# A four-image transformer step on one Trainium2 core: expert-sum transposes in the next step, attention units of one key range, scores in 64x64 tiles

## The chip, the core and the metric

The kernel runs on one core of one Trainium2 chip. The metric is the device time of one execution in microseconds (us), lower is better. Engine names are those of the profile: PE is TensorE's matmul and PEld its weight load, DVE is VectorE, ACT is ScalarE, POOL is GpSimd, SP is the queue of SyncE.

## What is computed

128 images of 176x208 pixels become 143 patches of 16x16 and one class token each, so 144 tokens of 128 channels. Three layers follow, each with a residual: a gated causal convolution layer, a layer with eight experts of which each token takes two, and (what this case is about) windowed attention and a layer that picks one of 16 weight matrices per image:

```python
qkv = (x @ w_qkv + b_qkv).reshape(B, S, 3, H, hd)      # H = 8 heads, hd = 16
q, k, v = (qkv[:, :, 0], qkv[:, :, 1], qkv[:, :, 2])
idx = jnp.arange(S)[:, None] + jnp.arange(-w, w + 1)[None, :]   # w = 32
valid = (idx >= 0) & (idx < S)
scores = jnp.einsum('bshd,bswhd->bshw', q, k_win) * scale
scores = jnp.where(valid[None, :, None, :], scores, -1000000000.0)
attn = jax.nn.softmax(scores, axis=-1)
out = jnp.einsum('bshw,bswhd->bshd', attn, v_win).reshape(B, S, D)
return out @ w_out + b_out
...
h = h + _L1_attn_ref(_layernorm(h, axis=-1), ...)
h = h + _L1_ffn_ref(_layernorm(h, axis=-1), ...)
```

## The kernel before

It has three stages. Stage A (to about 1150 us) takes the images through the first layer and the router of the experts and writes one row per token and chosen expert to DRAM. Stage B (to about 1800 us) runs the experts over blocks of 256 rows. Stage C (the last 1,250 us) is the one that the change touches. Channels lie on the partitions, tokens on the free axis; a step handles four images, 576 tokens, so there are 32 steps.

**A step of stage C is a software pipeline over five items.** `step(v, w, x, y, z)` is called on each engine with the item that entered now (`v`) and those that entered one to four steps earlier (`w`, `x`, `y`, `z`). The loop that calls it is `single_steps` on TensorE and `c_steps` on the others. Within a step the order of the instructions on each engine is written out by hand, and engines meet through semaphores alone.

- `v`: GpSimd gathers 12 rows of 96 tokens from `expert_out` into `ycho` by indirect DMA (L1429), multiplies them by the router's weights (L1437) and adds the two experts of each token into `ysum` (L1442). TensorE transposes `ysum` with six matmuls into the PSUM tile A0 (`moe`, L1488), as the last but one thing of its step.
- `w`: VectorE adds the residual (`prec`, L1845, the second thing in its step). Two layer norms follow (TensorE L1477 and L1482, ScalarE L1693 to L1699, VectorE L1894, L1900). The last instruction of VectorE's step writes the normalized `xq` (L1918).
- `x` and `y`: attention. `query_or_key` (L1494) projects `xq`, ScalarE writes `qs` (L1703) and `keys` (L1710), `values_in` (L1502) makes the values of each image and key range.
- `z`: the last layer with the matrix that VectorE picked for each image (`pick_expert`, whose last instruction is L1941, and L1825, the residual).

**Attention units.** The queries of an image are cut in 9 blocks of 16; each block sees one of three ranges of 96 keys, which start at 0, 32 and 48 (`STARTS`, `window`). Four blocks are a unit, nine units an item: before, unit `u` holds blocks 4u to 4u+3 of the 36 in order, so most units have blocks of two or three (image, range) pairs. Per unit:

- `diagonal` (POOL, L1450) spreads the queries into `qdiag`, two heads per 32 rows, 128x128 elements. It waits until the scores of three units earlier are done (a ring of three buffers). Two gathers or one follow each diagonal but the first.
- `scores` (PE) writes the band mask into a PSUM bank (L1515), then adds 16 matmuls, 4 blocks on 4 diagonal array tiles of 32x32 (L1519). An fp32 matmul has two records in the trace, so 32.
- `minimum` (DVE, L1805), `exps` (ACT, L1725), `turn` (PE transposes, L1529), `turned` (ACT, L1733).
- `values` (PE): softmax sums (L1542) and attention times values (L1554), four matmuls for each group of blocks that share an image and a range.
- `halves` and `heads` (DVE, L1812 to L1820): reciprocal, the choice of the right head, and the product, which goes to `att`.

The end of TensorE's step before reads:

```python
if x:
    scores(x, 8)
    turn(x, 6)
if v:
    if w:
        pe.wait_ge(norm4_act, w.upto(3, 2))
    ...
    moe(v, A0)
if x:
    values(x, 5)
```

and the end of VectorE's has `halves(x, 4)`, `residual(z)` (L1825), `heads(x, 4)` (L1817, L1820), `minimum(x, 7)` and the instruction for `xq`. `values(x, 5)` waits for L1817 of unit 4. The next step of TensorE begins with the query projection, which waits for `xq_ready`.

Of the kernel before, what the change touches and what calls it, by code (L numbers as in the profile page):

```python
# [22 lines left out]
ALU = mybir.AluOpType  # L23
# [22 lines left out]
HD = D // HEADS  # L46
WIN = 32
# [26 lines left out]
def window(b):  # L74

    return next(j for j, w in enumerate(STARTS)
                if w <= max(0, b * QB - WIN) and min(S, (b + 1) * QB + WIN) <= w + KW)

# [27 lines left out]
def const_tiles():  # L106
# [3 lines left out]
    for b in range(NQB):  # L110
        q = b * QB + np.arange(128) % QB
        key = STARTS[window(b)] + np.arange(KW)
        ok = abs(key[None, :] - q[:, None]) <= WIN
        band[:, b, :][ok] = 0.0
    band = np.concatenate([band, band[:, :UB - 1]], axis=1)
# [16 lines left out]
def build(nc, images, a):  # L132
# [8 lines left out]
    with ExitStack() as ctx:  # L141
# [65 lines left out]
        parity, pair_ones = sb("parity", [128, 2]), sb("pair_ones", [KW, 2, 2 * HD])  # L207
        place = [sb(f"place{s}", [G, 2 * NG], I32) for s in range(2)]
# [983 lines left out]
        def b_vector(v):  # L1192
# [35 lines left out]
            v.tensor_reduce(parity[:], C("head_rows").rearrange("p (t j) -> p j t", j=2), AX_X, ALU.add)  # L1228
            for j in range(2):
                v.memset(pair_ones[:, j, j * HD:(j + 1) * HD], 1.0)  # L1230
                v.memset(pair_ones[:, j, (1 - j) * HD:(2 - j) * HD], 0.0)
# [60 lines left out]
        qdiag, ex = ring_c("qdiag", [128, UB, 2, QB]), ring_c("ex", [128, UB, KW])  # L1292
# [38 lines left out]
        def blocks(u):  # L1331
            return [((u * UB + b) // NQB, (u * UB + b) % NQB) for b in range(UB)]
# [4 lines left out]
        def last_use(r):  # L1337

            return max(u for u in range(NU) if any((m * NWIN + window(qb)) // UB == r for m, qb in blocks(u)))
# [78 lines left out]
        def c_pool(pool):  # L1418
# [26 lines left out]
            def diagonal(x, u):  # L1445
                if u == 0:
                    pool.wait_ge(q_ready, x.upto(1, 1))
                if u >= RING or x.old(1):
# [3 lines left out]
                    qs[x.s][:, u * UB * QB:(u + 1) * UB * QB].rearrange("p (b q) -> p b q", b=UB).unsqueeze(2)  # L1452
                    .to_broadcast([128, UB, 2, QB]),
                    parity[:].unsqueeze(1).unsqueeze(3).to_broadcast([128, UB, 2, QB]),
# [15 lines left out]
        def c_tensor(pe):  # L1470
# [28 lines left out]
            def values_in(x, r, bank):  # L1499
                for w in range(UB):  # L1500
                    m, j = (r * UB + w) // NWIN, (r * UB + w) % NWIN
# [5 lines left out]
            def scores(x, u):  # L1507
# [6 lines left out]
                b0 = (u * UB) % NQB  # L1514
# [17 lines left out]
            def values(x, u):  # L1532
                need = max(m * NWIN + window(qb) for m, qb in blocks(u)) // UB
                if u in (0, 1, 3, 5):
# [11 lines left out]
                while b < UB:  # L1546
# [5 lines left out]
                    for t in range(NT):  # L1552
                        at = slice(t * PH, (t + 1) * PH)
                        done = nc.tensor.matmul(pv_bank()[at, b:b + c], val[:, m * NWIN + j, at],  # L1554
# [237 lines left out]
        def c_vector(v):  # L1792
# [22 lines left out]
            def heads(x, u):  # L1815
# [4 lines left out]
                v.tensor_tensor(att[:, u * UB * QB:(u + 1) * UB * QB].rearrange("p (b q) -> p b q", b=UB),  # L1820
# [16 lines left out]
            def step(v_, w, x, y, z):  # L1837
# [205 lines left out]
```

## Time and profile before

| what | value |
|---|---|
| runs of the kernel | 3069.62, 3073.66, 3074.09 us (median 3073.66) |
| the profiled execution: its own time | 3065.54 us |
| its span, first to last instruction | 3063.6 us |
| mean granted TensorE clock | 0.965 of full |
| busy: PE, PEld, DVE, ACT, POOL | 91%, 71%, 65%, 60%, 43% |
| DMA | 284.73 MB, mean 93 GB/s |

The busy shares are averages over three stages with different limits. In the profile's slices stage C is the last third: TensorE at nine tenths or more, VectorE at seven, ScalarE at six, GpSimd at five, DMA at one. How a step of it runs is read from the timeline of one step on each engine.

### The profile page before, as it was taken

What the parts mean: (1) busy time and instruction counts of PE and PEld (TensorE: products, weight loads), DVE (VectorE), ACT (ScalarE), POOL (GpSimd) and SP (SyncE); (2) the same over time, 40 slices, a digit from 0 to 9 for tenths busy, and PEclk for the clock granted to TensorE, in tenths of its full rate; (3) what the DMA queues carried; (4) which work ended last, traced back from release to release, by engine and by line L of the source; (5) the groups of instructions that cost most, each with busy time, mean ns of one, the idle gap of its engine ahead of it and who ended that gap; (6) DMA issues with size and microseconds to landing.
All of it is one profiled execution on the core that took longest, in us unless ns stands there. A gap on an engine that the chain in (4) does not pass through costs nothing.

```text
span 3063.6 us, 85773 instructions
## 1 busy us (share of the span) xinstructions
PE 2778.5 (91%) x31087; PEld 2160.1 (71%) x31087; DVE 1981.9 (65%) x4482; ACT 1844.8 (60%) x3693; POOL 1314.0 (43%) x1252
## 2 busy tenths in 40 slices
PE   6999999999999994899999968999999999999997
PEld 4666666666666663799999956777777777777775
DVE  4888888888888886222222215777777777777775
ACT  4776777777677774344444435666666666666664
POOL 1355555555655555000000026555555555555540
PEclk9999999999999997999999988999999999999998
DMA  3122222222222211677777741111111111111110
GB/s 130 70 78 95 85 83 83 77 77 77 89 90 83 83 32 52 211 231 226 228 230 229 229 141 39 54 50 46 46 47 46 46 45 47 46 45 45 46 34 28
DMA packets 139576, 284.73 MB, mean 93 GB/s; under 512 B 25440, under 2 KB 82784, under 8 KB 135392
## 3 DMA queue, kind: packets, MB, share of 16 engines
q1 hardware_dynamic: 114912, 245.77, 24.9%
q0 software_dynamic: 24576, 37.80, 4.5%
q8 instruction: 54, 0.88, 0.1%
q14 instruction: 34, 0.28, 0.0%
HBM read 215.18 MB, written 68.29 MB: 93 GB/s over the span
## 4 chain that ended last, share of the span: by engine, by line
issue 26%; PE 21%; POOL 10%; DMA 2%; ACT 1%; DVE 0%; POOLq 0%; SPq 0%; DVEq 0%; ACTq 0%
POOL ycho L1429 5%; PE psum L1519 4%; PE psum L1477 3%; PE psum L1494 3%; POOL ysum L1442 3%; PE psum L1502 2%; PE psum L1542 2%; PE psum L1529 2%; DMA ycho<-expert_out,place 2%; PE psum L1554 1%; POOL qdiag L1450 1%; PE psum L1515 1%; PE psum L1572 1%; PE psum L1482 1%; POOL ycho L1437 1%
## 5 line engine op out<-in xcount | busy, mean ns | idle before, releaser
L1429 POOL DMA_INDIRECT ycho<-expert_out,place x384 | 358.9, 935 | 664.7 <-issue 651.3
L1013 POOL DMA_INDIRECT expert_in<-rows,slot_i x384 | 445.3, 1160 | 130.5 <-issue 108.0
L1182 ACT ACTIVATE hid<-psum,w_blk 128x256 f32<-128x256 f32 x608 | 268.9, 473 | 326.9 <-PE psum L1139 326.9
L1725 ACT ACTIVATE ex<-psum,smin 128x96 f32<-128x96 f32 x1152 | 295.3, 341 | 158.2 <-DVE smin L1805 155.2
L483 PE MATMUL psum<-xn,w_in 128*128 128x288 f32 x1024 | 299.3, 416 | 31.7 <-ACT rf L697 27.7
L1450 POOL TENSOR_TENSOR qdiag<-qs,parity 128x128 f32<-128x128 f32 x288 | 117.7, 414 | 422.8 <-PE psum L1519 267.1
L1148 PE MATMUL psum<-w_blk,hid 128*128 128x128 f32 x2432 | 296.7, 275 | 0.0
L1812 DVE RECIPROCAL inv<-psum 128x64 f32<-128x64 f32 x288 | 159.0, 552 | 209.4 <-PE psum L1554 209.3
L1139 PE MATMUL psum<-x_t,w_blk 128*128 128x256 f32 x1216 | 289.5, 381 | 2.2 <-DMA w_blk<-w_exp_in 2.2
L989 POOL TENSOR_TENSOR unit<-unit 128x576 f32<-128x576 f32 x64 | 129.3, 2021 | 370.3 <-ACT unit L650 262.6
L1148 PEld LDWEIGHTS psum<-w_blk,hid 128*128 128x128 f32 x2432 | 283.9, 192 | 0.1
L483 PEld LDWEIGHTS psum<-xn,w_in 128*128 128x128 f32 x1024 | 187.2, 191 | 101.0 <-DVE xn L836 40.5
L1519 PE MATMUL psum<-keys,qdiag 32*32 32x96 f32 x9216 | 248.6, 244 | 0.0
L1519 PEld LDWEIGHTS psum<-keys,qdiag 32*32 32x32 f32 x9216 | 186.6, 104 | 76.5 <-issue 76.4
L1139 PEld LDWEIGHTS psum<-x_t,w_blk 128*128 128x128 f32 x1216 | 212.8, 191 | 34.2 <-DMA w_blk<-w_exp_in 2.6
L1733 ACT ACTIVATE ex_t<-psum 96x512 f32<-96x512 f32 x288 | 170.9, 593 | 106.4 <-PE psum L1529 106.2
L1246 DVE COPY x_t<-psum 128x256 f32<-128x256 f32 x152 | 64.5, 424 | 230.4 <-PE psum L1130 230.4
L1254 DVE TENSOR_TENSOR rows_out<-psum,w_blk 128x256 f32<-128x256 f32 x152 | 64.5, 424 | 215.8 <-PE psum L1148 215.8
L489 PE MATMUL psum<-xin,w_tok 128*128 128x286 f32 x768 | 195.0, 411 | 2.2 <-DVEq L453 2.2
L1805 DVE TENSOR_REDUCE smin<-psum 128x4 f32<-128x384 f32 x288 | 159.0, 552 | 49.9 <-PE psum L1519 48.6
L1529 PE MATMUL psum<-cst,ex 128*96 128x128 f32 x1152 | 180.0, 279 | 4.0 <-ACT ex_t L1733 2.0
L489 PEld LDWEIGHTS psum<-xin,w_tok 128*128 128x128 f32 x768 | 144.8, 192 | 50.6 <-issue 11.4
(237 smaller groups left out, 6031.7 us busy)
## 6 DMA issues: line engine op xcount, KB each, us to landing
w_blk<-w_exp_in SPq DMA_DIRECT2D x152, 578.0 KB, 4.0
xin<-x_in SPq DMA_DIRECT2D x32, 1716.0 KB, 7.2
rows_in<-expert_in SPq DMA_DIRECT2D x152, 128.0 KB, 2.4
expert_out<-rows_out SPq DMA_DIRECT2D x152, 128.0 KB, 3.3
h_dram<-h SPq DMA_DIRECT2D x32, 288.0 KB
x_dram<-x SPq DMA_DIRECT2D x32, 288.0 KB, 2.1
h1c<-h_dram SPq DMA_DIRECT2D x32, 288.0 KB, 3.0
x2c<-x_dram SPq DMA_DIRECT2D x32, 288.0 KB, 3.3
```

The costliest lines, as they stand in the source:

```text
L483: last = nc.tensor.matmul(bank[:, g, 0:T2], w, two(src)[:, g, :], start=True, stop=True)
L489: last = nc.tensor.matmul(bank[:, g, 0:2 * NPATCH], w_tok[:, k, :], xin[x.s][:, k, g * 2 * NPATCH:(g + 1) * 2 * NPATCH], start=(k == 0), s ...
L1013: pool.indirect_dma_start(out=expert_in[:, :], out_offset=bass.IndirectOffsetOnAxis(ap=slot_i[z.s][:, n:n + 1], axis=0), in_=rows[z.s][:, ...
L1139: nc.tensor.matmul(HB[b.s][c % HK], w_blk[b.q][:, c * 128:(c + 1) * 128], x_t[b.s][:], start=True, stop=True).then_inc(hid_done[b.s], 1)
L1148: last = nc.tensor.matmul(YB[b.s][:, t * 128:(t + 1) * 128], hid[b.s][:, c, t * 128:(t + 1) * 128], w_blk[b.q][:, FF + c * D:FF + (c + 1) ...
L1182: nc.scalar.activation(hid[b.s][:, c, :], HB[b.s][c % HK], ACT.Gelu_apprx_tanh, bias=w_blk[b.q][:, FF + FC * D + c:FF + FC * D + c + 1]).t ...
L1429: pool.indirect_dma_start(out=ycho[x.s][:, k, :], out_offset=None, in_=expert_out[:, :], in_offset=bass.IndirectOffsetOnAxis(ap=place[x.s] ...
L1519: done = nc.tensor.matmul(bank[at, b * KW:(b + 1) * KW], qdiag[u % RING][at, b, :, :].rearrange("p j q -> p (j q)"), keys[at, m, key_range ...
L1529: done = nc.tensor.transpose(XB[0:KW, b * 128:(b + 1) * 128], ex[u % RING][:, b, :], C("ident"))
L1725: done = nc.scalar.activation(ex[u % RING][:, b, :], score_bank(u)[:, b * KW:(b + 1) * KW], ACT.Exp, bias=smin[u % RING][:, b:b + 1], scal ...
L1733: nc.scalar.activation(ex_t[u % RING][:].rearrange("p b r -> p (b r)"), XB[0:KW, :], ACT.Copy).then_inc(ext_ready, 1)
L1805: v.tensor_reduce(smin[u % RING][:], score_bank(u).rearrange("p (b k) -> p b k", b=UB), AX_X, ALU.min).then_inc(min_ready, 1)
```

## The change

Three things are changed in stage C:

1. **The transposes of `ysum` (`moe`) move to the next step**, behind `values(y, 8)` and ahead of `scores(x, 1)`, for item `w` instead of `v`. `scores(x, 2)` follows `scores(x, 1)` at once and the small matmul `gates` comes after it. VectorE's `prec` moves behind the heads of unit 8.
2. **Units of one key range.** Units 0 to 7 are blocks 0 to 3 and 5 to 8 of each image, unit 8 is block 4 of all four images. `STARTS` stays; block 5 now takes the range at 48. Values are stored in the order `PLACES`, and the band mask in the order of `block_order`.
3. **Scores in 64x64 tiles.** `qdiag` holds four heads per 64 rows (`QH = 4`), 128x256 elements, masked by the new constant `quad` in place of `parity`. A unit has 4 blocks on 2 diagonal tiles of 64x64, 8 matmuls instead of 16.

```diff
+QH = 4
...
 def window(b):
-    return next(j for j, w in enumerate(STARTS)
-                if w <= max(0, b * QB - WIN) and min(S, (b + 1) * QB + WIN) <= w + KW)
+    return 0 if b < UB else 1 if b == UB else 2
...
+def block_order():
+    return list(range(UB)) + list(range(UB + 1, NQB)) + [UB] * IMGS
...
-        qdiag, ex = ring_c("qdiag", [128, UB, 2, QB]), ring_c("ex", [128, UB, KW])
+        qdiag, ex = ring_c("qdiag", [128, UB, QH, QB]), ring_c("ex", [128, UB, KW])
...
         def blocks(u):
-            return [((u * UB + b) // NQB, (u * UB + b) % NQB) for b in range(UB)]
+            if u == NU - 1:
+                return [(m, UB) for m in range(IMGS)]
+            return [(u // 2, (u % 2) * (UB + 1) + b) for b in range(UB)]
+
+        def unit_columns(t, u):
+            if u == NU - 1:
+                return four(t)[:, :, UB * QB:(UB + 1) * QB]
+            at = (u // 2) * S + (u % 2) * (UB + 1) * QB
+            return t[:, at:at + UB * QB].rearrange("p (b q) -> p b q", b=UB)
+
+        PLACES = [(m, j) for m in range(IMGS) for j in (0, 2)] + [(m, 1) for m in range(IMGS)]
...
                 pool.tensor_tensor(
                     qdiag[u % RING][:],
-                    qs[x.s][:, u * UB * QB:(u + 1) * UB * QB].rearrange("p (b q) -> p b q", b=UB).unsqueeze(2)
-                    .to_broadcast([128, UB, 2, QB]),
-                    parity[:].unsqueeze(1).unsqueeze(3).to_broadcast([128, UB, 2, QB]),
+                    unit_columns(qs[x.s][:], u).unsqueeze(2)
+                    .to_broadcast([128, UB, QH, QB]),
+                    quad[:].unsqueeze(1).unsqueeze(3).to_broadcast([128, UB, QH, QB]),
...
                 for b, (m, qb) in enumerate(blocks(u)):
-                    for t in range(NT):
-                        at = slice(t * PH, (t + 1) * PH)
+                    for t in range(HEADS // QH):
+                        at = slice(t * QH * HD, (t + 1) * QH * HD)
...
                     query_or_key(x, 0, A1)
-                    if w:
-                        pe.wait_ge(prec_ready, w.upto(1, 1))
                     values_in(x, 0, A0)
...
                 if y:
                     values(y, 8)
+                if w:
+                    if x:
+                        pe.wait_ge(k_ready, x.upto(1, 1))
+                    moe(w, A0)
                 if x:
                     scores(x, 1)
+                    scores(x, 2)
+                if w:
+                    pe.wait_ge(prec_ready, w.upto(1, 1))
                 if z:
                     gates(z, A0)
-                if x:
-                    scores(x, 2)
...
                     scores(x, 8)
                     turn(x, 6)
-                if v:
-                    if w:
-                        pe.wait_ge(norm4_act, w.upto(3, 2))
-                    elif v.old(1):
-                        pe.wait_ge(prec_ready, v.upto(1, 0))
-                    moe(v, A0)
                 if x:
                     values(x, 5)
...
-                if w:
-                    v.wait_ge(moe_done, w.upto(1, 1))
-                    v.wait_ge(h_landed[w.s], 32 * w.n + 32)
-                    v.tensor_tensor(two(prec[:]), both(A0), two(x2c[w.s][:]), ALU.add).then_inc(prec_ready, 1)
...
                     heads(y, 8)
+                if w:
+                    v.wait_ge(moe_done, w.upto(1, 1))
+                    v.wait_ge(h_landed[w.s], 32 * w.n + 32)
+                    v.tensor_tensor(two(prec[:]), both(A0), two(x2c[w.s][:]), ALU.add).then_inc(prec_ready, 1)
```

TensorE's order across the end of a step before: the band and score matmuls of unit 8 (L1515, L1519), `turn(x, 6)` (L1529), the transposes of `ysum` (L1488), `values(x, 5)` (L1542, L1554), then the next step's query projection (L1494):

```order
L1515 MATMUL psum<-band,ident_h 128x384
L1519 MATMUL psum<-keys,qdiag 32x96 x16
L1529 MATMUL psum<-cst,ex 96x128 x4
L1488 MATMUL psum<-cst,ysum 128x96 x6
L1542 MATMUL psum<-ex_t,pair_ones 32x64 x8
L1554 MATMUL psum<-ex_t,val 32x64 x8
```

In the changed kernel the transposes no longer stand there. They stand early in the step, where lines are shifted (L1563 and L1575 are `values`, L1509 the transposes, L1536 and L1540 `scores`, L1587 `gates`):

```order
L1563 MATMUL psum<-ex_t,pair_ones 32x64 x8
L1575 MATMUL psum<-ex_t,val 32x32 x16
L1507 ISA
L1509 MATMUL psum<-cst,ysum 128x96 x6
L1533 REGISTER_ALU
L1536 MATMUL psum<-band,ident_h 128x384
L1540 MATMUL psum<-keys,qdiag 64x96 x8
L1533 REGISTER_ALU
L1536 MATMUL psum<-band,ident_h 128x384
L1540 MATMUL psum<-keys,qdiag 64x96 x8
L1586 ISA
L1587 MATMUL psum<-gdiag,cst 128x4
```

They come behind `values(y, 8)`, whose four blocks now have four groups of 32 columns, and the score units 1 and 2 run back to back, each with 8 matmuls.

## Rows read from the trace of the kernel before

**Rows 1.** The page's first line.
```profile
span 3063.6 us, 85773 instructions
```
**Rows 2.** Table by stretch: length, busy time (instructions) of five engines, PE clock, DMA.
```profile
2200.00:2400.00 200.00, 187.49 (x3729) 141.17 (x3729) 147.72 (x366) 121.93 (x324) 110.35 (x120) 0.96 0.16 46
```
**Rows 3.** The list of waits, 2200 to 2600: us in total, times, longest.
```profile
POOL qdiag L1450 <- PE psum L1519: 78.8, 42, 3.8
...
PEld psum L1488 <- POOL ysum L1442: 25.9, 11, 2.4
```
**Rows 4.** Single lines, 2131 to 2960; L1442 in 1800 to 1950: ns min/median/max, first and last.
```profile
L1437 POOL TENSOR_TENSOR ycho<-ycho,weights x23: 2747/2749/2751, 2131.6 to 2956.9; 96x1536 f32<-96x1536 f32 x23
...
L1941 DVE TENSOR_SCALAR l<-l,m x23: 2540/2683/2752, 2131.6 to 2957.1; 4x16 f32<-4x16 f32 x23
...
L1442 POOL TENSOR_TENSOR ysum<-ycho x5: 1795/1803/2194, 1827.6 to 1949.1; 96x768 f32<-96x768 f32 x5
```
**Rows 5.** Timeline of PE, one step: start, us, instruction, [idle before <-releaser].
```profile
2362.07 0.71 PE L1488 MATMUL psum<-cst,ysum 96*128 96x96 f32 x6 [2.00 <-POOL ysum L1442]
...
2363.66 2.29 PE L1494 MATMUL psum<-xq,w_qkv 128*128 128x288 f32 x4
...
2389.30 0.43 PE L1542 MATMUL psum<-ex_t,pair_ones 96*32 96x64 f32 x16
...
2399.68 0.72 PE L1488 MATMUL psum<-cst,ysum 96*128 96x96 f32 x6 [2.17 <-POOL ysum L1442]
```
**Rows 6.** Timeline of POOL, the same step.
```profile
2389.48 0.40 POOL L1450 TENSOR_TENSOR qdiag<-qs,parity 128x128 f32<-128x128 f32 x1 [2.17 <-PE psum L1519]
...
2393.96 2.75 POOL L1437 TENSOR_TENSOR ycho<-ycho,weights 96x1536 f32<-96x1536 f32 x1 [1.76 <-DMA ycho<-expert_out,place]
2396.78 2.84 POOL L1442 TENSOR_TENSOR ysum<-ycho 96x768 f32<-96x768 f32 x1
```
**Rows 7.** Timeline of DVE, the same step.
```profile
2398.19 1.52 DVE L1820 TENSOR_TENSOR att<-one_head,inv 128x64 f32<-128x64 f32 x1
...
2400.10 0.74 DVE L1918 TENSOR_TENSOR xq<-psum,r 128x576 f32<-128x576 f32 x1
```
**Rows 8.** Timelines of DVE, POOL and PE, the step that ends at 2102.
```profile
2096.16 0.21 DVE L1941 TENSOR_SCALAR l<-l,m 4x16 f32<-4x16 f32 x1
...
2099.83 1.51 DVE L1820 TENSOR_TENSOR att<-one_head,inv 128x64 f32<-128x64 f32 x1
...
2096.21 2.78 POOL L1437 TENSOR_TENSOR ycho<-ycho,weights 96x1536 f32<-96x1536 f32 x1 [1.83 <-DMA ycho<-expert_out,place]
...
2101.32 0.72 PE L1488 MATMUL psum<-cst,ysum 96*128 96x96 f32 x6 [1.63 <-POOL ysum L1442]
...
2102.59 1.23 PE L1494 MATMUL psum<-xq,w_qkv 128*128 128x288 f32 x4
...
2126.97 0.43 PE L1542 MATMUL psum<-ex_t,pair_ones 96*32 96x64 f32 x16
```
**Rows 9.** Table by stretch, columns as in rows 2, behind the transposes of two steps.
```profile
2362.50:2366.00 3.50, 3.50 (x42) 2.59 (x41) 3.01 (x9) 1.52 (x6) 0.00 (x0) 0.55 0.74 252
...
2101.30:2105.00 3.70, 3.68 (x54) 3.09 (x54) 3.46 (x10) 2.43 (x7) 0.23 (x1) 1.00 0.77 247
```
**Rows 10.** PE from 2371.31 to 2371.40; then the chain that ended last: start, us, what.
```profile
2371.32 0.28 PE L1519 MATMUL psum<-keys,qdiag 32*32 32x96 f32 x4
...
2333.67 0.27 PE psum L1515
2333.94 0.79 PE psum L1519 x32
...
2336.14 0.23 PE psum L1554 x16
...
2343.15 0.22 PE psum L1554 x8
...
2344.54 0.16 PE psum L1515
```

More of the change, by code:

```diff
@@ L113, in const_tiles @@
         ok = abs(key[None, :] - q[:, None]) <= WIN
+        assert STARTS[window(b)] <= max(0, b * QB - WIN) and min(S, (b + 1) * QB + WIN) <= STARTS[window(b)] + KW
         band[:, b, :][ok] = 0.0
-    band = np.concatenate([band, band[:, :UB - 1]], axis=1)
+    band = band[:, block_order()]
     parts = {
@@ L207, in build @@
         parity, pair_ones = sb("parity", [128, 2]), sb("pair_ones", [KW, 2, 2 * HD])
+        quad = sb("quad", [128, QH])
         place = [sb(f"place{s}", [G, 2 * NG], I32) for s in range(2)]
@@ L1228, in b_vector @@
             v.tensor_reduce(parity[:], C("head_rows").rearrange("p (t j) -> p j t", j=2), AX_X, ALU.add)
+            v.tensor_reduce(quad[:], C("head_rows").rearrange("p (t j) -> p j t", j=QH), AX_X, ALU.add)
             for j in range(2):
@@ L1331, in blocks, with place_of @@
         def blocks(u):
-            return [((u * UB + b) // NQB, (u * UB + b) % NQB) for b in range(UB)]
+            if u == NU - 1:
[7 more added lines that the diff above has]
+        PLACES = [(m, j) for m in range(IMGS) for j in (0, 2)] + [(m, 1) for m in range(IMGS)]
+        def place_of(m, qb):
+            return PLACES.index((m, window(qb)))
         def key_range(qb):
@@ L1337, in last_use @@
         def last_use(r):
-            return max(u for u in range(NU) if any((m * NWIN + window(qb)) // UB == r for m, qb in blocks(u)))
+            return max(u for u in range(NU) if any(place_of(m, qb) // UB == r for m, qb in blocks(u)))
         class Single:
@@ L1500, in values_in @@
                 for w in range(UB):
-                    m, j = (r * UB + w) // NWIN, (r * UB + w) % NWIN
+                    m, j = PLACES[r * UB + w]
                     last = nc.tensor.matmul(bank[0:KW, 0, w * D:(w + 1) * D],
@@ L1513, in scores @@
                 bank = score_bank(u)
-                b0 = (u * UB) % NQB
+                b0 = 2 * UB if u == NU - 1 else (u % 2) * UB
                 nc.tensor.matmul(bank, ident_h[:], band[:, b0 * KW:(b0 + UB) * KW], start=True, stop=False)
                 for b, (m, qb) in enumerate(blocks(u)):
-                    for t in range(NT):
-                        at = slice(t * PH, (t + 1) * PH)
+                    for t in range(HEADS // QH):
+                        at = slice(t * QH * HD, (t + 1) * QH * HD)
                         done = nc.tensor.matmul(bank[at, b * KW:(b + 1) * KW],
@@ L1532, in values @@
             def values(x, u):
-                need = max(m * NWIN + window(qb) for m, qb in blocks(u)) // UB
-                if u in (0, 1, 3, 5):
+                need = max(place_of(m, qb) for m, qb in blocks(u)) // UB
+                if u in (0, 4, 8):
                     pe.wait_ge(val_ready, x.upto(NWIN, need + 1))
@@ L1553, in values @@
                         at = slice(t * PH, (t + 1) * PH)
-                        done = nc.tensor.matmul(pv_bank()[at, b:b + c], val[:, m * NWIN + j, at],
+                        done = nc.tensor.matmul(pv_bank()[at, b:b + c], val[:, PLACES.index((m, j)), at],
                                                 ex_t[u % RING][:, b:b + c, at].rearrange("p b (j q) -> p b j q", j=2),
@@ L1819, in heads @@
                 v.wait_ge(head_step, x.upto(HEAD * NU, HEAD * u + 3))
-                v.tensor_tensor(att[:, u * UB * QB:(u + 1) * UB * QB].rearrange("p (b q) -> p b q", b=UB),
+                v.tensor_tensor(unit_columns(att[:], u),
                                 one_head[:], inv[:], ALU.mult).then_inc(att_ready, 1)
```

## Prediction

> **What bounds the kernel now.** The profiled execution took 3065.54 us with a span of 3063.6 [rows 1], 8.1 us under the median of the three runs; I add my difference to the median, 3073.66. The change touches stage C only, the last 1,200 us. There TensorE is busy 187.5 us of 200 [rows 2], so the first thing to find is what its last 12.5 us wait for. The list of waits gives it: over 400 us TensorE's weight load stood 11 times, 25.9 us, before the expert-sum transposes, until GpSimd had written `ysum` [rows 3]. That is 2.4 us per step of four images. A step lasts 37.51 us: 23 products of the expert rows (L1437) start from 2131.6 to 2956.9, 825.3 / 22 [rows 4].
>
> The step is a loop. Take the one that ends at 2401. Let Q be the start of its query projection (2363.66) and s5 the end of its sixth score unit, where the next work starts (2389.30) [rows 5]. The timeline shows no gap between them: Q to s5 is 25.64. GpSimd's last diagonal waits for that unit; two gathers and their landing follow, and the product starts at 2393.96, s5 + 4.66 [rows 6]. The sum follows, and TensorE, done with `turn(x, 6)` and idle for 2.17, starts the transposes at 2399.68, 5.72 after the product began [rows 5]. From transposes to the next query it is 1.59 (2362.07 to 2363.66) [rows 5]. 25.64 + 4.66 + 5.72 + 1.59 = 37.61, the period of that step.
>
> Two more things are in these rows. First, VectorE is stopped by GpSimd: L1941, on 4x16 elements, takes 2683 ns as median of 23 [rows 4] and 0.21 in the one step where it began before the product [rows 8]; the product of 2.75 us covers it. L1820 takes 1.52 and ends with the sum [rows 7]. **`xq` is written two VectorE instructions later**, at 2400.10 plus 0.74 [rows 7]. Second, the idle time costs TensorE's clock: granted 0.55 just behind it, in 2362.5 to 2366, against 1.00 at the same place of the step at 2101.3 [rows 9], where it had been idle 1.63 us [rows 8]. So that is the 1.2 GHz level for most of the stretch, and its price is seen in Q to s5: 25.64 there, 2126.97 - 2102.59 = 24.38 in the other [rows 5, 8], 1.26 us; from transposes to Q it is 1.59 here and 2102.59 - 2101.32 = 1.27 there, another 0.32. In all 1.6.
>
> **The change, part by part.**
>
> *64x64 score tiles.* The instructions per unit go from 16 to 8 (records from 32 to 16), and one might book half of 0.79 us [rows 10]. But the records start in fours: in the first 0.09 us of a unit four have started [rows 10], one on each diagonal tile, and the fifth only later. A record streams the same 96 columns before and after, and each tile then has four blocks times two records, 8 in a row, in both kernels. 0.79 less about 0.11 of draining (0.27 to the first score record where the 0.16 of the same band matmul suffices elsewhere [rows 10]) is 0.68, or 8 x 0.085. Two tiles of 64x64 run 8 records each just as long. The weight load grows from 32 to 64 columns, but the transposes of `ysum` load 128 columns before moving 96, six in 0.72 with the tail [rows 5], so a load is hidden. I take **0**. Bounds: issue-bound, so down to half, -0.39; two tiles not side by side, +0.68. The first value is nearest to the fours seen. The Trainium skill, TensorEngine Tiling (Array Packing), section Instruction Overhead, gives about 60 cycles per matmul; as an estimate that is 32 x 25 ns = 0.80 per unit, as if the present unit were bound by issuing, and the new one would be bound by its columns. By it a unit would gain 0.1; the fours speak against it. This is a rival below.
>
> *Units of one key range.* The attention-times-value matmuls go from 18 groups to 12 per step. A unit of one group (8 records) takes 0.22, one of two groups (16) 0.23 [rows 10]: the columns are the same, four tiles share them. I take 0, at most -0.02 a unit; the last unit, with four groups, 0 to +0.2. Query columns are read at another stride, same length. The value tiles are released later (the second after unit 7, was 5), still before ScalarE comes to them.
>
> *Diagonals.* Nine GpSimd instructions per step grow from 128 to 256 elements. 0.40 now [rows 6]; the sum on 768 took 1.80 undisturbed [rows 4], so (1.80 - 0.40) / 640 = 2.19 ns per element: +0.28. By the product's slope (2.75 for 1536, 1.7 ns) +0.21, by doubling +0.40. GpSimd waits for scores 78.8 us in 11 steps [rows 3], 7.2 per step, and that hides eight of them (2.2 us; without the cover they would cost it). **One is on the path: the ninth, behind s5, +0.28.**
>
> *The transposes in the next step.* They leave the end of the step, and stand between `values(y, 8)` and `scores(x, 1)`, some 11 us later, long after the sum. The wait for `ysum` is gone, and the 0.72 moves into Q to s5: six records of 96 columns, 0.50 (0.45 to 0.72). Behind them `prec` (0.74 on VectorE, moved behind the heads of unit 8) must be ready before the gates, which now come after two score units of 1.05 each: 2.1 us against about 1.5, no wait. `minimum(x, 1)` is 0.7 later and is needed 2 us after that by `turn(x, 1)`; no cost.
>
> But what is late next? The query projection needs `xq`, and that stands on VectorE behind L1820, which ends with the sum. **So the wait for `ysum` is replaced by one for `xq`, about as late.** The product comes 0.28 later and L1941 then starts some 0.26 before it, so I take the other step's path: product 2096.21, query 2102.59, 6.38, with L1941 at 0.21, and L1820 at 1.51 again, ending with the sum at 2101.34 [rows 8]. The Trainium skill, SBUF — State Buffer, section SBUF: two separate sides, calls it an exclusive lock of the ports that VectorE and GpSimd share, held by whichever began first for its whole instruction; both steps agree.
>
> Sum at full clock: Q to s5 24.38 + 0.50, s5 to product 4.66 + 0.28, product to Q 6.38: 36.20. The same pieces of now, at full clock, are 24.38 + 4.66 + 5.72 + 1.27 = 36.03. TensorE is idle longer than now: it ends `turn` at 2399.68 - 2.17, s5 + 8.2, waits for VectorE's L1817 to run `values(x, 5)`, and waits again to s5 + 11.3, some 3 us in all less 0.6 of work. So the clock falls. It costs up to 1.6; but the fall may come before Q, and what passes at 1.2 GHz while nothing runs is free: down to 1.0. **37.2 to 37.8, middle 37.5 against 37.51.** Over 27 steps that are full (the five before are shorter and bound alike) -8 to +8 us; I put -2.
>
> **Rivals.**
> 1. *Scores bound by issuing.* 0.13 less for each of six units on the path, 0.8 per step, -21 us: 3052. For it: 0.79 / 32 is 25 ns. Against: the fours. 0.11.
> 2. *The clock stays up*, because the 0.6 of `values(x, 5)` cuts the idle time in two. 36.2, -1.3 x 27 = -35: 3038. For: the step at 2101 kept it after 1.63 us idle [rows 8, 9]. Against: 2.2 us sufficed 22 times, and now the two pieces together are longer. 0.13.
> 3. *VectorE isn't stopped*, so `xq` is early, and TensorE runs through: 37.51 - 2.2 idle - 1.6 clock + 0 = 33.7 by TensorE, but GpSimd's loop (4.94 + 4.6 behind s5) holds it at about 34.5, -3 x 27 = -80: 2993. Against: 23 of 23 steps. 0.07.
> 4. *Slower: L1941 stays behind the product.* It decides whether the product starts before it; now it does by 0.02. Then the sum takes 2.84 as now [rows 6], `xq` ends at product + 6.9 and Q is 0.6 later; with the clock's 1.6 the step is 38.4, +0.9 x 27 = +24: 3098. For: it is so in 23 steps, and VectorE's chain may slip with the longer diagonals. 0.15.
> 5. *The two 64x64 tiles don't overlap*: +0.68 on six units, 4.1 per step, +110: 3184. It is also how a change that doesn't do what it says would look. 0.05.
>
> **The numbers.** The forecast has 0.49: 3071.7, its own range 3065 to 3082. The range for 8 in 10 takes in rivals 1, 2 and 4: 3030 to 3101; rivals 3 and 5 stay out. 0.2% is 6 us, about what a measurement of this kernel can tell from no change. Faster: 0.31 of rivals 1 to 3 and 0.07 of the forecast's edge, 0.38. Slower: 0.20 and 0.06, 0.26. Same 0.36.
>
> **What would show it.** Right: products 37.2 to 37.8 apart; no wait of TensorE for `ysum`, and one of about 2 us before the query projection (L1515 after), released by VectorE's `xq`; a score unit still 0.79 and its records 0.28 for the first two or so; the diagonal 0.61 to 0.80; granted clock low once in each step. Wrong: a score unit under 0.7 (rival 1), clock at 1.00 throughout (2), no wait before the query (3), L1941's successor at 2.7 (4), a unit near 1.4 (5).

## The result, and the profile after

The changed kernel takes 3094.56 us (median of 6 runs, 3089.14 to 3099.66), the kernel before 3072.32 beside it (6 runs, 3067.89 to 3074.09). The ratio is 1.0075, 95% interval 1.0065 to 1.0086: slower by 0.75%. That is above the forecast's own range, 3065 to 3082, and inside the range for 8 in 10, 3030 to 3101; of the three directions "slower" had been given the smallest chance. The profiled execution took 3092.34 us, 26.8 more than that of before, with a span of 3090.5.

The products (L1458, L1437 before) start 38.52 us apart, 22 periods from 2134.6 to 2982.1; before it was 37.5 [rows 4]. One more microsecond in each of about 27 full steps is 27 us, the whole of the difference between the two profiled executions.

First the list of waits of the changed kernel, 2200 to 2600, in the columns of [rows 3]:

```profile
POOL qdiag L1471 <- PE psum L1540: 80.1, 41, 3.4
...
PEld psum L1515 <- DVE xq L1936: 23.1, 10, 2.3
...
PEld psum L1563 <- DVE one_head L1835: 9.2, 11, 0.9
```

The wait for `ysum` (25.9 us in [rows 3]) is gone. A wait for `xq` of 2.3 us per step (2.04 on the matmul side) stands in its place, and one of 0.8 (0.6) in front of `values(x, 5)`. That exchange was forecast. Next the timeline of TensorE over one step, as in [rows 5]:

```profile
2368.09 0.43 PE L1563 MATMUL psum<-ex_t,pair_ones 96*32 96x64 f32 x16 [0.53 <-DVE one_head L1835]
...
2370.77 2.29 PE L1515 MATMUL psum<-xq,w_qkv 128*128 128x288 f32 x4 [2.04 <-DVE xq L1936]
...
2382.41 0.71 PE L1509 MATMUL psum<-cst,ysum 96*128 96x96 f32 x6
...
2398.56 0.43 PE L1563 MATMUL psum<-ex_t,pair_ones 96*32 96x64 f32 x16
...
2407.42 0.43 PE L1563 MATMUL psum<-ex_t,pair_ones 96*32 96x64 f32 x16 [0.61 <-DVE one_head L1835]
...
2410.10 1.70 PE L1515 MATMUL psum<-xq,w_qkv 128*128 128x288 f32 x4 [2.04 <-DVE xq L1936]
```

Q is 2370.77, s5 is 2398.56, the next Q 2410.10: 27.79 and 11.54, where the step in [rows 5] had 25.64 and 11.97. GpSimd's timeline (as in [rows 6]) and VectorE's (as in [rows 7]) show the 11.54:

```profile
2398.73 0.61 POOL L1471 TENSOR_TENSOR qdiag<-qs,quad 128x256 f32<-128x256 f32 x1 [1.76 <-PE psum L1540]
2399.49 0.94 POOL L1450 DMA_INDIRECT ycho<-expert_out,place  x1
2400.74 1.36 POOL L1450 DMA_INDIRECT ycho<-expert_out,place  x1 [0.30 <-issue]
2403.80 2.75 POOL L1458 TENSOR_TENSOR ycho<-ycho,weights 96x1536 f32<-96x1536 f32 x1 [1.70 <-DMA ycho<-expert_out,place]
2406.63 2.20 POOL L1463 TENSOR_TENSOR ysum<-ycho 96x768 f32<-96x768 f32 x1
```

```profile
2403.22 0.21 DVE L1959 TENSOR_SCALAR l<-l,m 4x16 f32<-4x16 f32 x1
...
2404.43 2.74 DVE L1843 TENSOR_TENSOR outs<-outs,h 128x576 f32<-128x576 f32 x1
2407.09 0.27 DVE L1835 SCALAR_TENSOR_TENSOR one_head<-psum,parity,half 128x64 f32<-128x64 f32 x1
2407.40 1.52 DVE L1838 TENSOR_TENSOR att<-one_head,inv 128x64 f32<-128x64 f32 x1
2408.84 0.55 DVE L1823 TENSOR_REDUCE smin<-psum 128x4 f32<-128x384 f32 x1
2409.30 0.74 DVE L1936 TENSOR_TENSOR xq<-psum,r 128x576 f32<-128x576 f32 x1
```

The residual (L1843) starts during the product and ends behind it: 2.74 us for what takes 0.74 in the kernel before, where it starts behind the product. `one_head`, which `values(x, 5)` needs, stands behind it. L1838 is stopped by the sum and ends with it at 2408.8; `xq` comes two instructions later. TensorE's idle time at the end of the step looks like the shadow of these two instructions; e11_order tests that. The last gather takes 1.36 instead of 0.92 and pushes the product back.

Last, tables by stretch (columns as in rows 2): first 200 us, then two stretches behind the query of the step at 2370.77, and two behind that of 2410.10.

```profile
2200.00:2400.00 200.00, 187.05 (x2648) 138.72 (x2648) 138.09 (x354) 121.13 (x322) 115.39 (x121) 0.94 0.15 44
2370.50:2374.00 3.50, 3.23 (x10) 2.59 (x11) 1.84 (x7) 1.84 (x5) 0.00 (x0) 0.50 0.64 209
2374.00:2377.50 3.50, 3.50 (x36) 2.56 (x35) 0.76 (x3) 2.10 (x6) 3.17 (x5) 0.63 0.06 14
...
2409.90:2413.40 3.50, 3.30 (x13) 2.85 (x14) 1.76 (x7) 1.77 (x5) 0.66 (x2) 0.62 0.60 182
2413.40:2416.90 3.50, 3.50 (x43) 2.72 (x42) 1.17 (x4) 2.84 (x7) 3.05 (x4) 0.89 0.06 14
```

The clock falls about the query in each step, and in 6 of 22 steps the 1.2 GHz level lasts about twice as long (0.50 and 0.63 against 0.62 and 0.89). Those steps are 39.3 to 39.5 us, the others 38.0 to 38.4. In the six the clock fell 0.7 to 1.1 us ahead of the query, while TensorE stood idle; in the other 16 it fell between 0.6 us ahead of it and 0.9 behind.

**All steps together.** The pieces of the prediction, as means over the 22 or 23 steps with a product between 2130 and 2960, from the same rows (Q to s5, s5 to product, product to the end of `ysum`, product to the end of `xq`, product to the next Q), for the kernels that ran on chips that take about 3070 us for the kernel before:

| kernel | Q to s5 | s5 to product | to ysum | to xq | to next Q | step |
|---|---|---|---|---|---|---|
| before | 25.52 | 4.58 | 5.66 | 6.88 | 7.36 | 37.45 |
| changed | 27.02 | 5.21 | 5.03 | 6.25 | 6.30 | 38.52 |
| e1 move alone | 26.81 | 4.59 | 5.67 | 6.89 | 6.95 | 38.35 |
| e2 units alone | 25.76 | 4.57 | 5.66 | 6.88 | 7.24 | 37.57 |
| e3 tiles alone | 25.51 | 5.22 | 5.02 | 6.24 | 6.87 | 37.59 |
| e4 units and tiles | 25.97 | 5.23 | 5.02 | 6.24 | 6.67 | 37.87 |
| e12 changed, idle matmuls | 25.14 | 5.18 | 5.03 | 6.25 | 6.30 | 36.63 |
| e8 order alone | 24.37 | 4.53 | 4.64 | 4.79 | 5.96 | 34.86 |
| e16 move, order | 24.92 | 4.55 | 4.65 | 4.79 | 4.84 | 34.31 |
| e17 move, units, order | 24.96 | 4.57 | 4.64 | 4.78 | 4.84 | 34.37 |
| e11 changed, order | 25.18 | 5.16 | 4.65 | 3.82 | 3.87 | 34.22 |

### The profile page after: what moved, and what is told of

The parts are those of the page before. It is cut to its first block, busy times and chain, and to the rows that moved or that the text cites. A ratio compares the mean times of both kernels' runs of the same rounds, so it can differ in the third digit from the quotient of the medians.

```text
span 3090.5 us, 73493 instructions
## 1 busy us (share of the span) xinstructions
PE 2796.9 (90%) x24943; PEld 2158.8 (70%) x24943; DVE 1967.1 (64%) x4483; ACT 1851.0 (60%) x3693; POOL 1370.4 (44%) x1252
## 4 chain that ended last, share of the span: by engine, by line
PE 34%; issue 22%; DVE 2%; POOL 1%; ACT 1%; DVEq 0%; DMA 0%; SPq 0%; POOLq 0%; ACTq 0%
PE psum L1540 7%; PE psum L1498 5%; PE psum L1550 4%; PE psum L1523 4%; PE psum L1515 3%; PE psum L1563 3%; PE psum L1503 2%; PE psum L1575 2%; PE psum L1536 2%; PE psum L1593 1%; DVE xq L1936 1%; PE psum L1509 1%; DVE outs L1843 0%; POOL ycho L1450 0%; PE psum L1587 0%
## 5 line engine op out<-in xcount | busy, mean ns | idle before, releaser
L1450 POOL DMA_INDIRECT ycho<-expert_out,place x384 | 372.2, 969 | 659.7 <-issue 640.1
L1471 POOL TENSOR_TENSOR qdiag<-qs,quad 128x256 f32<-128x256 f32 x288 | 178.1, 623 | 395.0 <-PE psum L1540 263.7
L1540 PEld LDWEIGHTS psum<-keys,qdiag 64*64 64x64 f32 x4608 | 198.5, 133 | 78.5 <-issue 78.5
L1540 PE MATMUL psum<-keys,qdiag 64*64 64x96 f32 x4608 | 252.9, 249 | 0.0
```

The lines of the kernel that those rows point to most:

```text
L1450: pool.indirect_dma_start(out=ycho[x.s][:, k, :], out_offset=None, in_=expert_out[:, :], in_offset=bass.IndirectOffsetOnAxis(ap=place[x.s] ...
L1471: pool.tensor_tensor(qdiag[u % RING][:], unit_columns(qs[x.s][:], u).unsqueeze(2) .to_broadcast([128, UB, QH, QB]), quad[:].unsqueeze(1).u ...
L1540: done = nc.tensor.matmul(bank[at, b * KW:(b + 1) * KW], qdiag[u % RING][at, b, :, :].rearrange("p j q -> p (j q)"), keys[at, m, key_range ...
```

## The parts, one by one

These four kernels are pieces of the change itself: the diff stands ahead of the prediction, so only what each takes of it is named.

**e1_move**: the kernel before with the transposes and `prec` moved, nothing else.

> The kernel before with the transposes of ysum, the gates and prec moved as in the change, and nothing else. Theory T (the path runs query, sixth score unit, gathers, product, sum, xq; the wait for ysum is only exchanged for one for xq): query to sixth unit 24.2 + 0.55, unit to product 4.75 as before, product to end of sum 5.0 to 5.7, xq 1.3, together 35.8 to 36.5, and 1.0 to 1.8 for the clock: steps of 37 to 38, time 3060 to 3085, and a wait of about 2 us for xq ahead of the query projection. Rival M (the move alone makes the whole loss): steps of 38.5, 3094.

3089.47 us, ratio 1.0063 (1.0046 to 1.0080). On single lines from 2131 to 2960:

```profile
L1938 DVE TENSOR_SCALAR l<-l,m x22: 2587/2686/2807, 2134.2 to 2939.9; 4x16 f32<-4x16 f32 x22
...
L1442 POOL TENSOR_TENSOR ysum<-ycho x22: 2841/2847/2851, 2137.0 to 2942.6; 96x768 f32<-96x768 f32 x22
```

The last instruction of `pick_expert` is behind the product in all 22 steps, the residual therefore behind that, and it is the sum that takes 2.84. This is rival 4 as it was described, priced at a step of 38.4 and measured at 38.35. The time lies between theory T of the expectation (at most 3085) and rival M (3094, the move makes the whole loss), and the step is nearer to M's 38.5 than to T's 38. The move alone loses 0.90 us per step. By the table that is 0.55 of transposes in Q to s5 (24.37 to 24.92, e8 to e16, both at full clock), 0.74 more of clock there (26.81 - 24.92 against 25.52 - 24.37), and only 0.41 less between product and query.

**e2_units**: the new blocks, places and band order; 32x32 tiles; the transposes where they were.

> The kernel before with the units of one key range alone. T: the columns are the same, so no change, within 3 us of before (3072). A rival that books instructions would want about 0.1 us per step less, 3069, which this can't tell apart; one that holds the last unit's four groups or the later release of the values for the loss wants over 3080.

3069.87 us, ratio 0.9994 (0.9984 to 1.0003): no change, as forecast.

**e3_tiles**: `QH = 4`, `quad`, 64x64 tiles; old units, no move.

> The kernel before with the 64x64 score tiles alone (diagonals of 256 elements). T: the ninth diagonal is 0.21 longer and shifts the last gather into VectorE's two-input product of unit 3, so that it lasts 1.36 instead of 0.92: sixth unit to product 5.4 instead of 4.75; but L1941 then starts before the product, the sum ends 0.6 earlier. Steps of 37.5 to 38, time 3072 to 3085. Rival P (longer diagonals and tiles make the whole loss): 3094.

3080.80 us, ratio 1.0030 (1.0020 to 1.0040). The page gives the score records, and the lines the gathers:

```profile
L1522 PE MATMUL psum<-keys,qdiag 64*64 64x96 f32 x4608 | 252.8, 249 | 0.0
...
L1432 POOL DMA_INDIRECT ycho<-expert_out,place x265: 916/943/1385, 2131.2 to 2957.7; - x133
```

Half as many records, each 249 ns as before 244, and no shorter unit: 0.81 us from its first score record to the next instruction at full clock, 0.79 before. So halving the records gains nothing, and the two tiles do not stand behind each other. By the estimate from the Trainium skill (TensorEngine Tiling (Array Packing), Instruction Overhead), 32 records at about 60 cycles were the bound of the old unit and halving them would have gained 0.1 per unit; this run does not bear the gain out. What the tiles cost lies behind s5: +0.64 to the product, of which the diagonal is 0.21 and the last gather 0.43. They get the same 0.64 back between product and `ysum`, since `pick_expert` now ends ahead of the product. In the steady steps e3 loses only 0.14. Of its 15.3 us in the profiled execution, 5.5 are there before the first product (1830.3 against 1824.8; two executions of the changed kernel itself differ by as much, 1825.3 and 1831.3), 7.7 in the first five steps, which have only gathers and part of the pipeline, and 2 in all the rest.

**e4_nomove**: units and tiles, no move.

> The changed kernel with the transposes, the gates and prec put back where they were before (units and tiles stay). T: as the tiles alone, 3072 to 3085. Rival M: 3072 (the loss is in the move). Rival P: 3094.

3086.29 us, ratio 1.0046 (1.0029 to 1.0062), a little over the 3085 expected. The pieces are those of e3, with Q to s5 0.46 longer and less of a wait before the query. The changed kernel run again (**e10_after**) gave 3089.12, ratio 1.0063 (1.0046 to 1.0080), step 38.51. The move costs 0.90 per step on the old tiles (e1 less before) and 0.65 on the new ones (changed less e4); the tiles cost 0.14 alone and, with the units, 0.17 behind the move (changed less e1). Alone, the three parts cost 0.90, 0.12 and 0.14, 1.16 together, against the 1.07 of the whole. The two orders of TensorE hang on different things. With the move the query comes 0.05 behind `xq`, so the end of VectorE's step sets it. Without it (before, e2, e3, e4) it comes 0.36 to 0.63 behind `xq`: there the transposes and their wait for `ysum` set it.

## The clock: idle matmuls in the waits

**e12_filler** is the changed kernel with 20 bf16 matmuls per step into A0, which nobody reads; they lie in TensorE's two waits.

```diff
                     turn(x, 6)
+                if x and w:
+                    pe.wait_ge(norm4_act, w.upto(3, 2))
+                    busy(4)
                 if x:
                     values(x, 5)
+                if x and w:
+                    busy(16)
```

> The changed kernel with 20 matmuls per step whose result nobody reads, in TensorE's two waits at the end of a step (4 and 16). Theory: the fall of the clock costs 1.8 us of the changed step's 38.5, so the clock stays at 1.00 behind them, query projection to s5 comes to 25.0 instead of 26.5 to 27.7, and the step to 36.8: 27 x 1.7 = -46 us against the changed kernel, ratio about 0.985 of it. Rival: the matmuls stand in the way or the clock falls in spite of them; then query to s5 stays over 26 and the ratio is 1.00 or more.

> The changed kernel again, so that the two kernels behind it stand beside it on one chip. Theory: on a chip that runs the kernel before in 3072, 1.0075 of it, a step of 38.5 us, a granted clock of 0.960 over the run. If this chip is a slower one (before at 3147), the rival is that what makes it slow is a stall at the end of a step which the change could hide: then the ratio falls below 1.003.

On one chip: before 3069.98, e10_after 3089.12, e12_filler 3046.72, ratio to before 0.9922 (0.9905 to 0.9938), which is 42 us under the changed kernel. Timeline of TensorE at the end of a step, then its table by stretch:

```profile
2360.52 0.60 PE L1599 MATMUL psum<-band,ident_h 128*128 128x256 bf16 x4
2361.27 0.43 PE L1563 MATMUL psum<-ex_t,pair_ones 96*32 96x64 f32 x16 [0.15 <-DVE one_head L1844]
...
2361.86 1.92 PE L1599 MATMUL psum<-band,ident_h 128*128 128x256 bf16 x16
2363.96 1.24 PE L1515 MATMUL psum<-xq,w_qkv 128*128 128x288 f32 x4 [0.19 <-DVE xq L1945]
```

```profile
2200.00:2400.00 200.00, 198.23 (x2876) 147.74 (x2873) 147.37 (x374) 125.44 (x333) 122.52 (x125) 1.00 0.15 46
```

The query still starts 6.30 behind the product, so `xq` is as late as before. Only the clock is different: 1.00 in the 200 us of the table, and Q to s5 is 25.14 in all steps instead of 26.5 to 28.0. **The clock's share of the changed step is 38.52 - 36.63 = 1.89 us**, and 36.63 is its length at full clock. An earlier run of the same edit, **e5_filler**, fell on a slower chip (before 3147.5): 3122.79 where 3045 was expected, but the same ratio, 0.9921 (0.9897 to 0.9946).

## What stands ahead of xq

**e11_order** leaves TensorE and GpSimd of the changed kernel alone and writes the end of VectorE's step in another order: `heads` is cut into `one` (`one_head`) and `product` (L1838), and the two instructions that stop for GpSimd come behind `xq`.

```diff
-                if z:
-                    residual(z)
-                if x:
-                    heads(x, 4)
+                    one(x, 4)
                     minimum(x, 7)
...
+                if x:
+                    product(x, 4)
+                if z:
+                    residual(z)
```

> The changed kernel with VectorE's last instructions of a step reordered: what the query needs (xq) ahead of the product with r and of the residual, whose wait for the port costs the step 2.7 us. Theory: xq is early, ysum is written undisturbed in 1.8, TensorE's wait before the query falls from 2.04 to 0.5, the clock is back within Q to s5 at most once in some steps: step 36.5, 27 x 2.0 = -54 us against the changed kernel, ratio 0.982 of it, below the kernel before on any chip. Rival: the end of the step is bound by the clock alone and the order gives nothing beyond what idle matmuls give; then it stands within 0.2% of e12_filler.

2979.15 us, ratio 0.9702 (0.9686 to 0.9719): 110 us under the changed kernel, twice what was expected. Timelines of GpSimd, VectorE and TensorE:

```profile
2364.67 1.36 POOL L1450 DMA_INDIRECT ycho<-expert_out,place  x1 [0.30 <-issue]
2367.68 2.75 POOL L1458 TENSOR_TENSOR ycho<-ycho,weights 96x1536 f32<-96x1536 f32 x1 [1.65 <-DMA ycho<-expert_out,place]
2370.51 1.82 POOL L1463 TENSOR_TENSOR ysum<-ycho 96x768 f32<-96x768 f32 x1
```

```profile
2370.72 0.76 DVE L1939 TENSOR_TENSOR xq<-psum,r 128x576 f32<-128x576 f32 x1 [1.49 <-ACT r L1717]
2371.39 1.02 DVE L1844 TENSOR_TENSOR att<-one_head,inv 128x64 f32<-128x64 f32 x1
2372.34 0.75 DVE L1849 TENSOR_TENSOR outs<-outs,h 128x576 f32<-128x576 f32 x1
```

```profile
2371.53 1.24 PE L1515 MATMUL psum<-xq,w_qkv 128*128 128x288 f32 x4 [0.22 <-DVE xq L1939]
```

`xq` now waits for nothing of GpSimd, only for ScalarE's `r`, and ends 3.8 behind the product instead of 6.25. The residual takes its 0.75, and TensorE's idle time at the end of the step falls from 0.6 and 2.04 to 0.22. Of the 4.30 us that a step gains, 2.43 are the earlier query and 1.84 the clock, which stays at 1.00 without any filler. The expectation had 36.5, with a clock that still falls in some steps. The rival there, that idle matmuls give as much, is out by 68 us.

**e8_order_only** is the kernel before with that order.

> The kernel before with the same order of VectorE, nothing moved on TensorE, 32x32 tiles. Theory: the residual no longer stands between product and sum, so the sum takes 1.8 instead of 2.84, ysum is there 1.0 earlier, the idle time before the transposes falls from 2.2 to about 1.2 and the clock stays up: step 37.5 - 1.0 - 1.3 = 35.2, 27 x 2.3 = -62 us, ratio 0.980 of before. Rival: the move of the transposes is what makes the order worth anything (TensorE still waits for ysum, 1.2 us or more, and the clock falls as before): -1.0 alone, ratio 0.991.

2995.34 us, ratio 0.9762 (0.9745 to 0.9778), step 34.86. `ysum` comes 1.0 earlier behind the product, and in the list of waits, 2200 to 2600, TensorE's wait for it has become half as long:

```profile
PEld psum L1488 <- POOL ysum L1442: 14.0, 11, 1.4
```

Its Q to s5 is 24.37, the full clock. So the order is worth 2.6 us per step on its own, and this run shows what the wait for `ysum` in [rows 3] was: 1.3 of its 2.4 us remain with the sum undisturbed, and 1.1 came from the residual in the sum's way. `pick_expert` is still stopped by the product in nearly all steps and costs the sum nothing:

```profile
L1948 DVE TENSOR_SCALAR l<-l,m x24: 211/2612/2732, 2158.2 to 2956.6; 4x16 f32<-4x16 f32 x24
```

**e9_gather** is the changed kernel with `minimum(x, 6)` ahead of `heads(x, 3)`, so that L1838 of unit 3 comes behind the last gather.

> The changed kernel with the minimum of unit 6 ahead of the heads of unit 3 on VectorE, so that the two-input product of unit 3 comes some 0.5 us later, behind the last gather. T: the last gather takes 0.92 again instead of 1.36, sixth unit to product 4.95 instead of 5.4, time 3083 (3078 to 3089). Rival (the gather is held by the two-input instruction before, h2, or by DMA): gather 1.36, time 3094.

It ran on the slower chip: 3143.39 against 3147.5, ratio 0.9989 (0.9974 to 1.0005). Single lines:

```profile
L1450 POOL DMA_INDIRECT ycho<-expert_out,place x250: 916/943/995, 2131.1 to 2949.8; - x125
...
L1959 DVE TENSOR_SCALAR l<-l,m x21: 2268/2371/2544, 2157.2 to 2952.9; 4x16 f32<-4x16 f32 x21
...
L1463 POOL TENSOR_TENSOR ysum<-ycho x21: 2840/2847/2850, 2159.5 to 2955.3; 96x768 f32<-96x768 f32 x21
```

No gather is stretched and the product comes 4.79 behind s5, but `pick_expert` falls behind the product again and the sum takes 2.85, so the step gains nothing. It would be the answer if the changed kernel did otherwise on this chip. It does not: e5_filler, which has no such edit, has 259 gathers there with a longest of 956 ns, the product 4.78 behind s5 and `ysum` 5.68 behind the product. **This run is inconclusive** on its question. So what stretches the last gather is not shown. On the faster chips it takes 1.36 in all 22 steps of the changed kernel, of e3 and of e11, and 0.92 in all of before, e1 and e2. L1838 of unit 3 lies beside it in each of the long ones (it starts 0.80 into the gather). But the same instruction lies beside 33 other gathers of the changed kernel between 2130 and 2960, most often from 0.85 on, and none of these takes over 0.96. Another instruction of VectorE with two operands in SBUF, L1918, starts 0.24 ahead of each long gather, where in e1 it starts 0.03 ahead of the short one and in e5 0.29 behind its start. No run parts the two. What e5 and e9 do show is how little decides it: the two ends of the step, a stretched gather with an early `pick_expert` and a short gather with a late one, are one chip apart, and both bring `xq` at nearly the same distance from s5, 11.5 and 11.7.

## The order with parts of the change

With the order mended, which part of the change gains? The first of these runs fell on slower chips:

> The changed kernel with the end of VectorE's step in another order: head choice of unit 4, minimum of unit 7, xq, and only then the two instructions that read two SBUF operands (the product of unit 4 and the residual of z). T: xq no longer waits for GpSimd's sum, TensorE starts the query about 9 us after the sixth score unit instead of 11.7, its idle time is under 1 us, the clock stays up: steps of 34 to 35, time 2975 to 3000. Rival (TensorE waits for xq because the norm's ScalarE part is late, not because of the port): 3085 or more.

> The move alone (32x32 tiles and units as before) with the same order of VectorE's end as e6. T: as e6, and the shorter diagonals don't matter once GpSimd isn't on the path: 2970 to 2995, within 8 us of e6. Rival (GpSimd's chain still sets the step): 15 us or more under e6, by the 0.6 between sixth unit and product.

> The move of the transposes and the order of VectorE, 32x32 tiles and the old units. Theory: with the order, the move takes the transposes (0.72 and the wait of 1.2) from the end of the step and puts 0.55 into it: against the order alone 34.9 - 1.17 + 0.4 + 0.5 = 34.6 or less, ratio to before 0.974 or less. Rival: the move needs the longer path of the 64x64 tiles to show no loss; on the other chip the same kernel stood at 0.9953 with steps of 39.2, and then it does so here: over 0.985.

> Move, units of one key range and the order, score tiles left at 32x32: what e11_order is without its tiles. Theory: the 64x64 tiles cost 0.6 in query to s5 and 0.6 behind s5, less what they save in product to ysum only where the residual was in the way, so without them the step of 34.2 becomes 33.4 to 33.8: ratio to before 0.965. Rival: the tiles have a part in the gain of e11_order that the traces so far don't show; then this one is slower than it, 0.975 or more.

> The changed kernel with VectorE's order again, for comparison on this chip: 0.970 of before if this chip runs before in 3070, 0.9715 if it is the slower one (3147).

On the chips that take 3147 to 3150 for before: changed with order 3058.11 and 3060.27 (e6_order, e15_order: ratios 0.9715, 0.9690 to 0.9740, and 0.9722, 0.9688 to 0.9755); without the tiles 3129.01 (e14_small_order: 0.9930, 0.9908 to 0.9952); without tiles and units 3131.79 and 3132.60 (e7_move_order, e13_move_order: 0.9953, 0.9937 to 0.9970, and 0.9941, 0.9921 to 0.9960). Nothing came out as expected but e15_order. e6_order and e7_move_order miss the 2970 to 3000 that both expectations had, and e7_move_order is 74 us over e6_order instead of within 8. For e13_move_order and e14_small_order the rivals came true: there the 64x64 tiles, which were to cost, are worth 2%. The list of waits of e14_small_order, 2200 to 2600, has lines that the faster chips do not show:

```profile
DVE gate_bc L1886 <- remote: 25.5, 10, 2.6
...
DVE smin L1820 <- remote: 17.0, 19, 1.8
```

"remote" is a release that the trace ties to no instruction. Where VectorE waits 1.8 us for the scores it starts 1.5 us after TensorE's last score matmul has ended. e15_order has such lines too, on other instructions. The same two kernels again:

> e13_move_order again, in the hope of a chip that runs the kernel before in 3070. There: step of 34.6 or less, ratio 0.974 or less, if the move itself gains with that order; over 0.980 if it does not.

> e14_small_order again, likewise. On a chip that runs before in 3070: if the 64x64 tiles only cost, the step is 33.4 to 33.8 and the ratio 0.965 against the 0.970 of e11_order; if they have a part in its gain, 0.972 or more.

These ran on the faster kind (before 3070.41). e16_move_order: 2973.36, ratio 0.9686 (0.9668 to 0.9704). e17_small_order: 2973.14, ratio 0.9680 (0.9664 to 0.9696), with a step of 34.37, over the theory's 33.4 to 33.8 and under the rival's ratio of 0.972. So there, with the order:

- the move gains: 0.9762 to 0.9686, step 34.86 to 34.31. The transposes leave the end (5.96 to 4.84 behind the product) and cost 0.55 in Q to s5;
- the units do nothing, 0.9680;
- the tiles do nothing that can be told, 0.9702: +0.22 in Q to s5 (0.09 of it in the score records of six units), +0.59 to the product, and an `xq` that no longer depends on where the product is, so that the step is 34.22.

All three beat the kernel before on both kinds of chip. Which of them is best depends on the chip: e11_order is level on the faster ones and ahead by 2.2% on the slower ones.

## Why the prediction was wrong

**The forecast's mechanism held.** No wait for `ysum`, a wait of 2.04 before the query released by `xq`, L1959 at 0.21, L1838 at 1.52 ending with the sum, a score unit of 0.81, the diagonal 0.61: so it was forecast, and so it came. Its step was 37.5; measured 38.52. The miss of 1.0 is in terms that were sized too small: 0.59 in the clock, the larger part, and 0.43 at full clock, most of it the last gather and the tiles.

- **Q to s5, 24.38 + 0.50 = 24.88.** Measured 25.14 at full clock (e12). The move is 0.55 (24.37 to 24.92, e8 to e16), as taken. The tiles, taken as 0, are about 0.2 (24.96 to 25.18, e17 to e11). The score records have 0.09 of that, 0.81 for 0.79 in each of six units.
- **s5 to product, 4.66 + 0.28 = 4.94.** Measured 5.21 in the changed kernel and 4.58 before. The diagonal was smaller than taken (0.21, by the product's slope). What was left out is the last gather, +0.43: with the longer diagonals it starts 0.2 later against VectorE's work and takes 1.36 for 0.92. That the tiles bring this is shown (e3 has it, e1 and e2 do not), which of VectorE's instructions does it is not. The prediction asked of each longer instruction what it delays, and not what it then lies next to.
- **Product to Q, 6.38.** Measured 6.30. The price of the path by the other step [rows 8] was right, and the escape of `pick_expert` that it counts on came in all 22 steps (to `ysum` 5.03 for 5.66).
- **Clock, 1.0 to 1.6, 1.3 taken.** Measured 1.89. This is the step that failed most. In 16 of 22 steps the fall costs 1.55 (Q to s5 is 26.69 for 25.14), the full price that the prediction had read from [rows 5, 8]; the discount of 0.3, for a part that would pass while TensorE is idle, was not there. In the other 6 steps the longer fall costs 2.74 (27.88), which the sum had not; that is 0.3 more per step. At the full price the sum would have been 37.8, slower than the kernel before. What makes the longer fall stays open. The changed step has a second idle piece, 0.6 in front of `values(x, 5)`, and before, with one piece of 2.1, never had the longer fall in 23 steps; but e4_nomove, also with one piece of 2.1, has it in 2 of 22 steps, and e1_move, with two pieces, in 5 of 22.
- **The rest, -2 us.** It was put in without a row; the sum's middle was level with the kernel before. The difference of the medians is 22.2 us, of the two profiled executions 26.8.

**The rivals.** 1 (a gain, since scores are bound by issuing) and 5 (tiles in turn) fall with e3, where a unit takes 0.81 us for 0.79. 2 and 3 are not what the changed kernel did, and e12 and e11 show what each was worth: the clock alone 1.89 us per step, against 1.3 in the forecast; VectorE not stopped 4.3, a step of 34.2 where rival 3 had 34.5. Rival 4 gave nearly the measured time (38.4, 3098), but that is luck: it is the mechanism of e1 and not of the changed kernel, where L1959 took 0.21 in 22 of 22 steps.

**Where the expected gain went.** Behind the product the query is 1.06 earlier (7.36 to 6.30). The move gives 0.41 of that (e1), the rest comes with the tiles, by which `pick_expert` ends ahead of the product. Nothing of it is left since Q to s5 grew by 1.50, of which 0.77 (25.14 - 24.37) is work and 0.7 more of clock than before, and s5 to product by 0.63. Of that 0.7, some 0.3 the kernel before paid ahead of the query, inside its 7.36 (1.59 for 1.27 from transposes to query [rows 5, 8]).

## What to carry to other kernels

When a wait at the end of a loop is taken away, look at what the next step's first instruction needs and which engine writes it. If that engine is stopped by the same neighbour as the old wait, the move alone may lose: here it gave 0.6% away with the residual ahead of `xq` and gained 0.8% with it behind (e8_order_only to e16_move_order). The cure was to write two instructions whose results are needed later behind the one that the next step starts with. Price a clock that has fallen at its full rate, and measure it with idle matmuls before building on it.

## What the runs showed that was not expected

- The stopped party in [rows 4, 7] was VectorE; it can be GpSimd too. The sum takes 2.20 in the changed kernel and 1.82 in e11: in the changed one it begins, at 2406.63, while the residual with its two operands in SBUF still runs, to 2407.17. The Trainium skill, SBUF — State Buffer, section SBUF: two separate sides, names an instruction of VectorE with two SBUF inputs as one that can take the shared ports and block a GpSimd instruction that reads SBUF; the trace agrees for the sum.
- A gather's issue by GpSimd takes 1.36 us for 0.92 at one place of each step, with the larger diagonals alone (e3). Its cause is open, as told under e9_gather.
- 20 matmuls that compute nothing made the changed kernel 1.4% faster (3089.12 to 3046.72).
- Two kinds of chip: before takes 3070 to 3072 on some and 3147 to 3150 on others, and the order of kernels is not the same on them. What makes the others slower stays open. It is not the granted clock: the changed kernel with idle matmuls has a step of 38.78 there (e5_filler) and 36.63 on the faster kind (e12_filler), with the clock at 1.00 from 2200 to 2400 in both. There is no trace of the kernel before from one, only late "remote" releases, of VectorE and ScalarE above all, in its variants. Since the changed kernel itself was not run on one, its 1.0075 holds for the faster kind.
